# Solving all sixteen heads of a chunk in four 64x64 quarters of TensorE, the solution by products with identity plus the power

## The reference

```python
def step(Sst, inp):
    q_t, k_t, v_t, g_t, b_t = inp
    Sst = Sst * jnp.exp(g_t)[..., None, None]
    kv = jnp.einsum('bhkv,bhk->bhv', Sst, k_t)
    delta = (v_t - kv) * b_t[..., None]
    Sst = Sst + k_t[..., None] * delta[..., None, :]
    o = jnp.einsum('bhkv,bhk->bhv', Sst, q_t)
    return (Sst, o)
...
mixed = jax.nn.silu(y).transpose(0, 2, 1)      # y: causal convolution, 4 taps, over q, k, v
g = -jnp.exp(A_log) * jax.nn.softplus(a + dt_bias)
...
_, o = jax.lax.scan(step, S0, xs)
h_ = o * jax.nn.silu(z)
```

## Time and profile before

| what | us |
|---|---|
| median of 3 runs | 4654.08 (4645.75 to 4654.64) |
| span of the profiled execution | 4621.9 |
| busy in it: PE | 3777.9 |
| DVE | 2632.5 |
| ACT | 1833.3 |
| POOL | 1182.1 |

### The profile page before, as it was taken

One profiled execution on the slowest core, in us unless ns is written; L12 is line 12 of the kernel. 1 busy time (PEld: TensorE's weight loads), 2 busy tenths in 40 slices (PEclk: granted clock), 3 DMA queues, 4 the chain that ended last, 5 costly groups with the idle time before them and its releaser, 6 DMA issues. The chain is left out here.

```text
span 4621.9 us, 133260 instructions
## 1 busy us (share of the span) xinstructions
PE 3777.9 (82%) x60410; PEld 2904.4 (63%) x60410; DVE 2632.5 (57%) x4402; ACT 1833.3 (40%) x2937; POOL 1182.1 (26%) x1148
## 2 busy tenths in 40 slices
PE   5888989889898898988989999915777887777855
PEld 4877878778687787877878888812333433433424
DVE  5355454544545445454335555544877888888743
ACT  2333333333333333323336666613444454444422
POOL 2131421314213142231345555361000000000063
PEclk9999999999999999999989999957898889898878
DMA  6341000000000000000044444321212222222214
GB/s 198 134 142 41 24 25 11 24 23 26 17 10 21 7 16 18 8 19 7 15 142 161 154 152 155 102 56 42 60 47 51 61 56 51 56 60 53 57 33 132
DMA packets 206516, 284.72 MB, mean 62 GB/s; under 512 B 86712, under 2 KB 148416, under 8 KB 199808
## 3 DMA queue, kind: packets, MB, share of 16 engines
q1 hardware_dynamic: 136160, 111.25, 9.4%
q0 software_dynamic: 24016, 107.80, 7.1%
q10 hardware_dynamic: 45776, 57.15, 3.7%
HBM read 215.59 MB, written 72.61 MB: 62 GB/s over the span
## 5 line engine op out<-in xcount | busy, mean ns | idle before, releaser
L874 DVE TENSOR_TENSOR sd_z<-psum,sd_z 128x512 f32<-128x512 f32 x320 | 219.0, 689 | 415.5 <-PE psum L742 415.0
L2784 PE MATMUL psum<-ss_h,ident 128*128 128x512 f32 x512 | 297.2, 710 | 24.1 <-DVE ss_h L2899 23.6
L2893 DVE TENSOR_TENSOR_SCAN ss_h<-ss_da,ss_h 128x1024 f32<-128x1024 f32 x128 | 294.1, 2298 | 3.5 <-ACT ss_da L2833 3.0
L921 POOL TENSOR_TENSOR sd_z<-id,s_up 128x512 f32<-128x512 f32 x64 | 81.3, 1270 | 812.8 <-DVE s_up L880 812.2
L2541 POOL TENSOR_TENSOR at_qs<-at_q,slot_of 128x512 f32<-128x512 f32 x32 | 45.6, 1435 | 951.3 <-ACT at_q L2411 706.8
L1802 PE MATMUL psum<-e_h,e_mid_w 128*128 128x256 f32 x1248 | 283.8, 381 | 1.0 <-ACT e_h L1846 1.0
L1802 PEld LDWEIGHTS psum<-e_h,e_mid_w 128*128 128x128 f32 x1248 | 238.4, 191 | 34.0 <-ACT e_h L1846 1.6
L742 PE MATMUL psum<-sd_z,s_do 64*64 64x64 f32 x6144 | 223.8, 227 | 30.1 <-ACT s_do L823 28.6
L742 PEld LDWEIGHTS psum<-sd_z,s_do 64*64 64x64 f32 x6144 | 205.9, 142 | 64.8 <-issue 33.8
L742 PE MATMUL psum<-s_low,s_up 64*64 64x64 f32 x6144 | 225.1, 225 | 24.9 <-DVE sd_z L874 22.3
L2454 ACT ACTIVATE x_tok<-psum 128x512 f32<-128x512 f32 x320 | 165.2, 603 | 192.4 <-PE psum L2379 192.2
(11 more groups left out here) (472 smaller groups left out, 9883.7 us busy)
## 6 DMA issues: line engine op xcount, KB each, us to landing
ss_rows<-bc_scratch SPq DMA_DIRECT2D x128, 512.0 KB, 4.9
answered<-ce_zeros ACTq DMA_DIRECT2D x19, 1024.0 KB
routed<-ce_zeros ACTq DMA_DIRECT2D x16, 1024.0 KB, 9.1
st_eg<-gate_scratch SPq DMA_DIRECT2D x128, 128.0 KB, 5.2
table_mid<-in_t_mid ACTq DMA_DIRECT2D x4, 1536.0 KB
m_w<-in_m_w ACTq DMA_DIRECT2D x16, 256.0 KB, 7.7
table_down<-in_t_down ACTq DMA_DIRECT2D x1, 2560.0 KB
g_x<-in_x SPq DMA_DIRECT2D x8, 256.0 KB, 6.0
```

The source lines that it names most:

```text
L874: dve.tensor_tensor(d.z[:, :, :], bank[:, :].rearrange("p (a t) -> p a t", a=NP), d.z[:, :, :], ALU.add).then_inc(T.dve.give(r, name), 1)
L921: pool.tensor_tensor(D[m % 3].z[:, :, :], w["id64"][:, :].unsqueeze(1).to_broadcast([P, NP, C64]), T.up[:, :, :], ALU.subtract).then_inc(T ...
L2784: t = pe.matmul((b5, b6)[m][:, :], w["ident"][:, :], Z.h_of(b, n)[:, m, :], start=False, stop=(n == DS - 1), skip_group_check=True)
L2893: dve.tensor_tensor_scan(flat, flat2(Z.da[n % 2][:, :, :]), flat, 0.0, ALU.mult, ALU.add).then_inc(Z.dve.give(b, f"s{n}"), 1)
```

## The change

A power's `up` and `low` now stand in one tile (`powers`, 128 x 2 x 8 x 64), and a line's two PSUM banks are used as one (`pair`). `crossed` replaces `product`: it is again 16 matmuls, but of each group of four, two (j of 0) write the half of the partitions that they read, and two (j of 1) write the other half, into the line's other bank. So the four of a group use the four quarters of the array. The heads with j of 1 change sides at each product; `SLOT_HEADS` and the views of `by_key` put the pairs of heads that share a key at j of 0 and 1, and VectorE writes their first z, I - up, crosswise, in two instructions on 64 partitions (c0, c1), while GpSimd makes the other half (s0).

The solution is no longer added to: z becomes (I + low) z, one product, copied out of PSUM by ScalarE (`chain`). GpSimd adds the identity to `low` in place (i1 to i4), after the square that reads it; VectorE does it for the last one, out of PSUM (i5). A square's two products lie in the two halves of the pair of banks, and ScalarE takes both with one copy of 128 x 1024 (`power`). The z product goes into the same half as the next square's `up`, so that square waits for the copy of z.

For a chunk there are again 14 products. ScalarE has 4 copies of 1024 and 5 of 512 where it had 9 of 512; VectorE has c0, c1 and i5 where it had 5 additions; GpSimd has s0 and four instructions i1 to i4 where it had one. A chunk takes 13 rounds of its line.

```diff
@@ -47,7 +47,7 @@
-SLOT_HEADS = [4 * g + s for g in range(NG) for s in (0, 2, 1, 3)]
+SLOT_HEADS = [4 * g + 2 * u + j for j in range(2) for g in range(NG) for u in range(2)]
...
@@ -288,23 +288,30 @@
-    PE = ["ea", "eo", "kq", "kt", "low1", "up2", "low2", "z1", "up4", "low4", "z2", "up8", "low8", "z3", "up16", "low16", "z4", "low32", "z5"]
-    ACT = ["da", "do", "low1", "up2", "low2", "up4", "low4", "up8", "low8", "up16", "low16", "low32"]
-    DVE = ["up", "at", "kd", "z1", "z2", "z3", "z4", "z5"]
-    POOL = ["z0"]
...
+    PE = ["ea", "eo", "kq", "kt", "low1", "sq1", "sq2", "z1", "sq3", "z2", "sq4", "z3", "sq5", "z4", "z5"]
+    ACT = ["da", "do", "low1", "p1", "p2", "z1", "p3", "z2", "p4", "z3", "z4", "z5"]
+    DVE = ["up", "at", "kd", "c0", "c1", "i5"]
+    POOL = ["s0", "i1", "i2", "i3", "i4"]
...
+        self.pair = C.psum[:, 2 * n:2 * n + 2, :]
+        self.powers = [sb(f"s{n}_powers{i}", [P, 2, NP, C64]) for i in range(2)]
+        self.da, self.do = self.powers[1][:, 0, :, :], self.powers[1][:, 1, :, :]
+        self.last_low = self.powers[1][:, 0, :, :]
...
-        def product(bank, left, right, name):
-            for p in range(NP):
-                for u in range(2):
-                    t = pe.matmul(bank[half(u), p * C64:(p + 1) * C64], left[half(u), p, :], right[half(u), p, :], start=True, stop=True)
-            t.then_inc(T.pe.give(r, name), 1)
+        def crossed(region, left, right):
+            for g in range(NG):
+                for j in range(2):
+                    for u in range(2):
+                        out = T.pair[half(u ^ j), j, region * HALF + g * C64:region * HALF + (g + 1) * C64]
+                        t = pe.matmul(out, left[half(u), j * NG + g, :], right[half(u), j * NG + g, :], start=True, stop=True)
+            return t
+        def square(n):
+            up, low = T.power(n - 1)[:, 0, :, :], T.low(n - 1)
+            if n < 5:
+                crossed(0, low, up)
+            crossed(1, up, low).then_inc(T.pe.give(r, f"sq{n}"), 1)
+        def chain(n):
+            crossed(0, T.last_low if n == 5 else T.low(n), z).then_inc(T.pe.give(r, f"z{n}"), 1)
         if m % NCHUNK < 2:
             pe.wait_ge(*G.pool.at(b, "blo"))
         if r:
-            pe.wait_ge(*T.dve.at(r - 1, "z5"))
+            pe.wait_ge(*T.act.at(r - 1, "z5"))
         exponents(bx, "mask_a", b3, "ea")
-        if r:
...
-        yield
-        was(T.act, "up4")
-        was(T.act, "low4")
-        product(bx, T.low, z, "z2")
-        product(by, T.low, T.up, "up8")
-        was(T.dve, "z2")
-        product(bx, T.up, T.low, "low8")
-        yield
-        was(T.act, "up8")
-        was(T.act, "low8")
-        product(by, T.low2, z, "z3")
-        product(bx, T.low2, T.up2, "up16")
-        was(T.dve, "z3")
-        product(by, T.up2, T.low2, "low16")
-        yield
-        was(T.act, "up16")
-        was(T.act, "low16")
-        product(bx, T.low, z, "z4")
-        product(by, T.up, T.low, "low32")
-        yield
-        was(T.act, "low32")
-        was(T.dve, "z4")
-        product(bx, T.low2, z, "z5")
+        square(1)
+        yield
+        was(T.act, "p1")
+        square(2)
+        yield
+        was(T.act, "p2")
+        was(T.pool, "i1")
+        was(T.dve, "c1")
+        chain(1)
+        yield
+        for n in (3, 4):
+            was(T.act, f"z{n - 2}")
+            square(n)
+            yield
+            was(T.act, f"p{n}")
+            was(T.pool, f"i{n - 1}")
+            chain(n - 1)
+            yield
+        was(T.act, "z3")
+        square(5)
+        yield
+        was(T.dve, "i5")
+        was(T.pool, "i4")
+        chain(4)
+        yield
+        was(T.act, "z4")
+        chain(5)
         go.solved[T.n] = r
         yield
...
+        z = D[m % 3].z
+
+        def power(n):
+            act.wait_ge(*T.pe.at(r, f"sq{n}"))
+            act.activation(T.power(n)[:, :, :, :].rearrange("p r (j g) t -> p r j (g t)", j=2),
+                           T.pair.rearrange("p j (r x) -> p r j x", r=2), ACT.Copy).then_inc(T.act.give(r, f"p{n}"), 1)
+
+        def chain(n):
+            act.wait_ge(*T.pe.at(r, f"z{n}"))
+            act.activation(z[:, :, :].rearrange("p (j g) t -> p j (g t)", j=2), T.pair[:, :, 0:HALF], ACT.Copy).then_inc(T.act.give(r, f"z{n}"), 1)
...
-            dve.tensor_tensor(d.z[:, :, :], bank[:, :].rearrange("p (a t) -> p a t", a=NP), d.z[:, :, :], ALU.add).then_inc(T.dve.give(r, name), 1)
...
+        dve.wait_ge(*T.dve.at(r, "up"))
+        for u in range(2):
+            dve.tensor_tensor(d.z[half(1 - u), NG:NP, :], w["id64"][half(u), :].unsqueeze(1).to_broadcast([64, NG, C64]), up[half(u), NG:NP, :],
+                              ALU.subtract).then_inc(T.dve.give(r, f"c{u}"), 1)
+        for _ in range(8):
+            yield
+        dve.wait_ge(*T.pe.at(r, "sq5"))
+        dve.tensor_tensor(T.last_low.rearrange("p (j g) t -> p j g t", j=2), T.pair[:, :, HALF:2 * HALF].rearrange("p j (g t) -> p j g t", g=NG),
+                          w["id64"][:, :].unsqueeze(1).unsqueeze(1).to_broadcast([P, 2, NG, C64]), ALU.add).then_inc(T.dve.give(r, "i5"), 1)
+        yield
+        yield
...
+            return w["id64"][:, :].unsqueeze(1).to_broadcast([P, n, C64])
+
+        def one_low(n):
+            pool.wait_ge(*T.pe.at(r, f"sq{n + 1}"))
+            pool.tensor_tensor(T.low(n), T.low(n), one(NP), ALU.add).then_inc(T.pool.give(r, f"i{n}"), 1)
+        yield
         yield
         pool.wait_ge(*T.dve.at(r, "up"))
         if m >= 3:
             pool.wait_ge(*V.pe.at(m - 3, "tx"))
-        pool.tensor_tensor(D[m % 3].z[:, :, :], w["id64"][:, :].unsqueeze(1).to_broadcast([P, NP, C64]), T.up[:, :, :],
-                           ALU.subtract).then_inc(T.pool.give(r, "z0"), 1)
-        for _ in range(7):
-            yield
+        pool.tensor_tensor(D[m % 3].z[:, 0:NG, :], one(NG), T.power(0)[:, 0, 0:NG, :], ALU.subtract).then_inc(T.pool.give(r, "s0"), 1)
+        yield
+        yield
+        one_low(1)
+        yield
+        yield
+        one_low(2)
+        yield
+        yield
+        one_low(3)
+        yield
+        yield
+        one_low(4)
+        yield
+        yield
         go.solved[T.n] = r
         yield
```

More of the change, by code:

```diff
@@ L849, in solve_act @@
         yield
-        copy(T.low2, by, "low32")
+        chain(4)
         yield
+        chain(5)
         go.solved[T.n] = r
@@ L1708, in solved_marks @@
             yield
-        for _ in range(8):
+        for _ in range(12):
             yield
```

99 lines of the change are left out of this document (34 added, 65 removed).

## The result

| | median, us | ratio to before, 95% interval |
|---|---|---|
| before | 4654.36 (4645.75 to 4666.5) | |
| the change | 4436.14 (4430.5 to 4441.3) | 0.9527 (0.9511 to 0.9542) |

The change is faster by 218 us; 4415 had been forecast, with a range of 4300 to 4710. The profiled execution took 4431.32 us with a span of 4429.5. So 1.8 us lie around a span.

The account below looks back on a forecast made before the run. TensorE was taken to bound a batch's first two turns, TensorE and VectorE the others. Turns summed to -33.9 us, less 4 for the clock: -29.9, times 8 is -239; span 4383, plus 32: 4415 us, range 4300 to 4710.

Parts of the forecast that it names:

- The main term: TensorE's 64x64 products overlap in four quarters: 0.47 us a product in place of 0.94, 52.6 us a batch.
- The row of layer 1 with four columns: Profile row of a product putting 32 instructions into four columns at once, 27 ns each; the ground for 0.47 us.
- Both rivals on a product's pace: Quarters don't overlap further: 0.87 us a product, 4710, chance 0.20; starts no closer than 25 ns: 0.80 us, 4654, chance 0.08.
- Additions: TensorE's waits for VectorE's additions to z go away: 6.8 us a batch.
- The chain's waits: TensorE stands between squares and z products for GpSimd's identities and ScalarE's copies: 5 us a turn, covered in the fourth.
- kg and the splits: TensorE stands 2.87 us a turn for kg behind GpSimd's identity, less beside w_qkv blocks; GpSimd's splits add 6 us a batch.
- The clock: TensorE stands more, so its granted clock falls after such stretches: 4 us a batch given back.
- The rival on the clock: A quarter of the time at 1.2 GHz in place of a tenth: 25 us a batch added, 4610; chance 0.08.
- The turns: Four turns of a batch change by -4.4, +0.7, -12.6 and -17.6 us.
- The sum: Turns together -33.9 us a batch, -29.9 after the clock's 4; times 8 batches is -239.
- The first rival: Quarters don't overlap further and GpSimd's place in the chain remains: +7 us a batch, 4710, slower; chance 0.20.

Follow-up runs that it names:

- uncrossed kernel: The change with the crossing alone undone, so every product writes the half of the partitions that it reads; ratio 0.9975 to before, 4645.4 us.
- long row shown: Row of 12 further crossed products once a batch, added to the change, their output overwritten; 4491.21 us from a single execution.
- own tile: The change with GpSimd's identity plus low written into a separate tile for each line, not in place; ratio 0.9410 to before.
- z on VectorE: The change with the five copies of z a chunk made by VectorE in place of ScalarE; ratio 0.9604 to before.

## Why the prediction was right, and where its steps were not

**The main term held.** A product was forecast at 0.47 us and takes 0.48 to 0.50; the 52.6 us a batch are 51.5. The uncrossed kernel shows that this is the overlap of the quarters and nothing else. The row of layer 1 with four columns was the right one to argue from. Both rivals on a product's pace fell: 0.87 by the earlier trace rows read as a pace of instructions, and 0.80. Of the latter, the Trainium skill's section "Wait — 56ns, not 53.3ns?" in "TensorE: Matmul & The Clock Gate" says that starts come no closer than about 25 ns; the trace does not agree, they average 14.6 ns over 128 instructions. What is true is that in the long row shown the mean is 27 to 29 ns, by the supply.

**Additions.** -6.8 us a batch forecast, 41.5 / 6 = 6.9 measured.

**The chain's waits** were right in size and half wrong in owner. In the profile, identities add 5.0 us a batch, and ScalarE's copies 39.4 + 34.0 - 24.5 = 48.9 in six batches, 8.2; the forecast had 15 for both, nearly all on GpSimd. (The identities' waits were to be some 100 us in the whole profile; they are 44.3.) The own tile shows that the two are in series: with GpSimd out, ScalarE is late next.

**kg and the splits** were mis-sized: 10.6 + 6 us a batch were forecast, the rise is 8.3 - 3.9 = 4.4. TensorE waits for kg three times a batch, not four: 3.9 us at the end of the first turn, where the router's indirect DMA of 0.98 us is added to the 2.87 of the forecast, 1.7 at the end of the second, where the splits stand, 2.7 at the end of the third, which is the forecast's value, and not at all in the fourth. The splits show at most in one wait for an identity in the second turn, 2.9 us at its longest. The 3.9 of before should have been taken off.

**The clock** was to give back 4 us. It is 44.4 - 32.4 = 12 us more of a batch at the lower level, 6 lost. The rival on the clock had the mechanism and too large a size: 17% of the time is at the lower level, not 25%. Its sum was off as well: a further 15% of a batch of 259 us at the lower level loses half of its work, 19 us, not 170 x 0.15 = 25.

**The turns** were the step that failed. Means of six batches:

| turn | before | uncrossed | the change | change of the time: forecast | measured |
|---|---|---|---|---|---|
| 1 | 60.4 | 69.1 | 61.2 | -4.4 | +0.8 |
| 2 | 62.0 | 72.2 | 65.8 | +0.7 | +3.8 |
| 3 | 77.3 | 73.7 | 65.6 | -12.6 | -11.7 |
| 4 | 88.3 | 72.2 | 66.7 | -17.6 | -21.6 |

The forecast left the gates' matmuls and the blocks with w_qkv in the turns where they had been. But a chunk takes 13 rounds now, so more rounds of projection fit beside a turn. The counts of MATMULs by turn say it: 1495, 1509, 1611 and 1589 before, 1529, 1630, 1543 and 1523 after. In the batch shown, turn 2 has got all 96 of the gates' small MATMULs, which stood in turn 3, and 12 of the 32 of w_qkv that stood there; 16 of the 24 of w_z have gone from turn 4 to turn 3, and one product of 32 from turn 4 to turn 1. In the uncrossed kernel, whose products are as long as before, turns 1 and 2 grow by 9 and 10 us, and 3 and 4 shrink by 4 and 16. In turn 2 that is moved work (PE is busy 9.0 us more), in turn 1 mostly standing (6.2 us more, 4.0 for kg among it). All turns are alike now, and in the first the crossing just pays for that.

In turn 1 TensorE stands 13.2 us where it stood 4.2, 3.9 of it for kg and 1.9 for issue. That is 9.0 more and was forecast, 8.8. What the forecast of this turn missed is the clock (11.9 us at the lower level in place of 6.3, 2.8 lost) and the product that came in. In turn 4 it had 19.6 us of standing, and 12.1 came. It also took the third and fourth turn of before from one batch, 73.6 and 90.6, where the means are 77.3 and 88.3.

**The sum.** -28.9 us a batch against -29.9 is better than its parts, and that is luck: waits for kg and the splits that were 12 us too dear paid for the clock and for issue, which was in no term. One more step was wrong: times 8. The last batch has nothing left to project and stays as it was, 181.2 us for its last seven chunks before and 178.3 after. (In the uncrossed kernel they take 193.1: with no projection to fill the waits, the rest of the change costs 12 us there and the crossing gives 15.) From the first chunk's solution to the last's the gain is 2205.4 - 2000.5 = 205 us. What follows is the same code and took 14 us more in the trace after; in the other eleven kernels it took 2 to 22 us more than in this trace of before, alike for kernels that ran on one chip (13 to 22, 2 to 4, 2 to 4). So it seems to go with the chip and not with the kernel; no run tests that.

**The first rival's price** was wrong too. Had a product not become faster, the time would have been not 4710 or more but that of the uncrossed kernel, 0.9975 of before: no change. Its terms for kg, the splits and the chain were too large; the relief of VectorE, put at 3 us a batch, was 5.6.

## What to carry to other kernels

Small fp32 matmuls (64x64 here) went twice as fast in four quarters, with pairs that write the other half of the partitions alternating with those that don't; but count instructions as well as array time, since in long rows the supply of instructions set the pace. When the busiest engine gets faster, read the order of the engines that it then waits for: one instruction of GpSimd moved behind kg was worth 1.3%, and a fill-in of useless matmuls only what the missing wait and its half clock had cost. Measure the part that carries the gain apart from the rest: here z by products, with all that came along, was worth 0.25%. And when a kernel is slower with no more waiting, as with z on VectorE, look at the time at the lower clock.

## What the runs showed of the hardware that was not expected

- Instructions reach TensorE in transfers of 16 KB, 256 instructions, and in the long row shown TensorE begins the next 256 every 3.47 to 3.76 us: 27 to 29 ns for a MATMUL with its load, whatever the array could do (14.6 ns with four quarters). Two quarters at 29 ns use nearly all of it. In ordinary rounds, too, 56 of 72 gaps under issue end 1.15 to 1.65 us after such a transfer has landed.
- MATMULs on four quarters start 14.6 ns apart on average: four within some 20 ns, and the next four 58 ns after the first of these.
- In the batch of the change from 1190.5 to 1446.1 us the clock fell to the half eight times: six times during or just behind a wait of 2.4 to 5.2 us, and twice in the fourth turn, where the waits around it were 1.2 to 1.7 us. A stretch of 6.8 us at 0.50 was at 1.00 with 1.9 us of matmuls put into the wait.
